# Two-piece expert passes regrouped by array width, down weights moved from a copy to a DMA, scatters and last sums rearranged

## The reference

```python
logits = h @ gate_w.T
scores = softmax(logits); topk_w, topk_idx = top_k(scores, 6)
for e in range(16):
    g = h @ w_gate[e].T          # 256 -> 176
    u = h @ w_up[e].T
    out = silu(g) * u @ w_down[e].T   # 176 -> 256
    y = y + cw[:, e:e + 1] * out
```

## Time and profile before

| | us |
|---|---|
| median of 3 runs (lowest to highest) | 876.45 (874.01 to 876.85) |
| the profiled execution, whole | 867.91 |
| its span (first to last instruction) | 866.1 |
| first pass of the last stage begins (T of pass 2) | 638.70 |
| last `pair_y` ends | 846.46 |

### The profile page before, as it was taken

How to read it: one execution, slowest core, us unless ns; L and a number is a source line. 1 busy time by engine, 2 the same in 40 slices (tenths; PEclk the granted TensorE clock), 3 DMA queues, 4 the chain that set the end, 5 groups by cost and what they waited for, 6 DMA issues and landing times.

```text
span 866.1 us, 15945 instructions
## 1 busy us (share of the span) xinstructions
PE 789.5 (91%) x5107; PEld 521.6 (60%) x5107; DVE 507.1 (59%) x1270; ACT 400.1 (46%) x856; POOL 278.8 (32%) x374
## 2 busy tenths in 40 slices
PE   5988799889979998999999999899899999999990
PEld 3566566676557785777777767667654444444440
DVE  5999876666512236756556655777534763443564
ACT  3987777555123333443233342232527454555540
POOL 3643744113500033111111111137602265554430
PEclk9998999999989999999999999999979999999995
DMA  4002770181253221044453533113232243537316
GB/s 140 2 1 37 244 257 2 35 238 51 80 165 109 86 67 56 19 142 134 134 159 122 171 92 78 53 50 101 90 68 68 62 126 116 135 117 245 101 46 212
DMA packets 103590, 91.22 MB, mean 105 GB/s; under 512 B 38104, under 2 KB 95448, under 8 KB 103512
## 3 DMA queue, kind: packets, MB, share of 16 engines
q1 hardware_dynamic: 93288, 67.92, 27.2%
q0 software_dynamic: 6912, 19.28, 6.4%
q10 hardware_dynamic: 3312, 3.02, 1.0%
HBM read 50.47 MB, written 38.67 MB: 103 GB/s over the span
## 4 chain that ended last, share of the span: by engine, by line
PE 62%; DVE 12%; issue 6%; POOL 5%; DMA 4%; ACT 3%; DVEq 0%; ACTq 0%; SPq 0%; POOLq 0%
PE bank L1383 8%; PE bank L1346 7%; PE bank L673 7%; PE bank L1240 6%; PE bank L1226 5%; PE bank L699 5%; PE bank L896 3%; PE bank L2166 3%; POOL rows L771 3%; PE bank L918 2%; PE bank L657 2%; PE bank L2123 2%; PE bank L2150 2%; DMA rows<-arena,sidx 2%; PE bank L685 2%
## 5 line engine op out<-in xcount | busy, mean ns | idle before, releaser
L1487 ACT ACTIVATE arena<-bank 128x512 f32<-128x512 f32 (+1 forms) x96 | 46.9, 525 | 147.5 <-PE bank L1346 147.4
L1138 POOL TENSOR_TENSOR arena<-arena,causal_t 128x256 f32<-128x256 f32 x64 | 45.1, 726 | 214.0 <-ACT arena L1492 214.0
L781 POOL DMA_INDIRECT ret<-arena,ridx x64 | 66.1, 1033 | 103.9 <-ACT arena L747 49.9
L673 PE MATMUL bank<-arena 128*64 (+1 forms) x512 | 91.0, 477 | 1.0 <-DVE arena L733 1.0
L1383 PEld LDWEIGHTS bank<-arena 128*128 128x128 f32 x640 | 76.6, 192 | 5.2 <-POOL arena L1138 2.7
L1383 PE MATMUL bank<-arena 128*128 128x129 f32 x640 | 77.5, 276 | 1.7 <-POOL arena L1138 1.7
L1346 PE MATMUL bank<-arena 128*128 128x512 f32 (+3 forms) x256 | 75.7, 440 | 1.4 <-DVE arena L1546 1.4
L699 PE MATMUL bank<-arena 88*64 (+1 forms) x512 | 69.8, 393 | 3.2 <-DVE arena L725 1.7
L754 DVE TENSOR_TENSOR arena<-arena,bank 128x176 f32<-128x176 f32 x64 | 21.6, 337 | 86.2 <-ACT arena L741 86.0
L1240 PE MATMUL bank<-arena 128*128 128x256 f32 x256 | 62.6, 389 | 1.5 <-DVE arena L1553 1.5
L1240 PEld LDWEIGHTS bank<-arena 128*128 128x128 f32 x256 | 49.4, 194 | 22.6 <-issue 12.1
(11 more groups left out here) (288 smaller groups left out, 1527.0 us busy)
## 6 DMA issues: line engine op xcount, KB each, us to landing
rows<-arena SPq DMA_DIRECT2D x16, 544.0 KB, 4.6
rows_in<-place SPq DMA_DIRECT2D x5, 1664.0 KB, 14.4
arena<-rows SPq DMA_DIRECT2D x64, 128.0 KB, 2.1
arena<-in_w_gu SPq DMA_DIRECT2D x24, 256.0 KB, 3.5
arena<-ret SPq DMA_DIRECT2D x12, 512.0 KB, 6.7
arena<-in_w_dn SPq DMA_DIRECT2D x24, 176.0 KB
arena<-in_wq SPq DMA_DIRECT2D x32, 128.0 KB, 3.9
arena<-in_wo SPq DMA_DIRECT2D x32, 128.0 KB, 2.0
```

Of the source, the lines that this page charges most:

```text
L673: mm = nc.tensor.matmul(p_gu[J % 2][u * HR:(u + 1) * HR, 0:2 * FE].rearrange("p (y n) -> p y n", y=2), pxT[:, J % 2, k, u * HR:(u + 1) * H ...
L781: nc.gpsimd.indirect_dma_start(ret[h], bass.IndirectOffsetOnAxis(ap=ridx[:, h, j:j + 1], axis=0), py[J % NY], None).then_inc(s_ret, 16)
L1138: nc.gpsimd.tensor_tensor(blocks, blocks, causal_t[:].unsqueeze(1).to_broadcast([P, 2, P]), ALU.mult).then_inc(s_p, 1)
L1487: nc.scalar.activation(th[:, sbank * 512:sbank * 512 + w], b_s[sbank][:, 0:w], ACT.Tanh, scale=SCALE / SOFTCAP).then_inc(s_th, 1)
```

## The change

Six edits belong to it:

1. The PE order of pass J becomes `T(J+2), H(J-1), G(J+1), D(J-1)`: the two transposing groups stand together and the two 64-wide groups stand together. DVE's order becomes `pair_h(J-1), pair_mul(J+1), pair_y(J-1)`, then the routing part.
2. `pair_copy_dn` is gone. `load_dn_pair` on SP loads the second piece's down weights from HBM (176 KB), with the row number read from the table, four steps behind `load_rows`.
3. `pair_y` moves from ACT to DVE. Most routing parts of half 1 are called one pass earlier.
4. `send_rows` takes ranges: half 0 sends five scatters in each of heads 25 to 28 and four in head 29 (was four in each of heads 25 to 30). Half 1 sends groups of six (was four).
5. `rows1_back(0)` moves from pass 1 into head 31, ahead of `pair_x(0)`.
6. Of the last sums, tiles 0 and 1 stay as `add_back` on DVE. For tiles 2 and 3 DVE builds 12 diagonal matrices (`spread_weights`, passes 40 to 45), and PE sums with them in PSUM (`sum_back`); DVE then adds that to x.

```diff
         def rows1_table(self, dve, h):
...
-            for y, w in enumerate((GU1, 2 * DIM)):
-                nc.vector.tensor_scalar(tab1[:, h, y, :], c.ej, float(E1 - 1), float(w), ALU.min, ALU.mult).then_inc(s_tab, 1)
+            nc.vector.tensor_scalar(tab1[:, h, 0, :], c.ej, float(E1 - 1), float(GU1), ALU.min, ALU.mult).then_inc(s_tab, 1)
+            for u, w in enumerate((2 * DIM, FE)):
+                nc.vector.tensor_scalar(tab1[:, h, 1, :].rearrange("p (j u) -> p u j", u=2)[:, u, :],
+                                        c.ej.rearrange("p (j u) -> p u j", u=2)[:, u, :], float(E1 - 1), float(w),
+                                        ALU.min, ALU.mult).then_inc(s_tab, 1)
...
-            pe.wait_ge(s_wbd, J + 1)
+            pe.wait_ge(s_wbd[J % 2], wbd_0[J % 2] + 16 * (J // 2 + 1))
...
-        def pair_y(self, act, J):
+        def pair_y(self, dve, J):
...
-            nc.scalar.copy(py[J % NY], p_y).then_inc(s_pye, 1)
+            nc.vector.tensor_copy(py[J % NY], p_y).then_inc(s_pye, 1)
...
+        def spread_weights(self, dve, k):
+            if k == 0:
+                dve.wait_ge(s_rows, SC + 2 * SC1)
+            for t in (2, 3):
+                ins = nc.vector.scalar_tensor_tensor(out=dg[:, 2 * k + t - 2, :], in0=ident[:], scalar=wk1[:, 1, k, t:t + 1],
+                                                     in1=ident[:], op0=ALU.mult, op1=ALU.mult)
+        def sum_back(self, pe):
+            pe.wait_ge(s_rx1, 3)
+            for k in range(K1):
+                pe.wait_ge(s_ys[k], ys_0[k] + 32)
+                for t in (2, 3):
+                    mm = nc.tensor.matmul(b_y[0][:, (t - 2) * DIM:(t - 1) * DIM], dg[:, 2 * k + t - 2, :], ys[k][:, t, :],
+                                          start=(k == 0 and t == 2), stop=(k == K1 - 1), skip_group_check=True)
+        def load_dn_pair(self, sp, J):
+            off = self.owner(sp, J, 1, 1)
+            if J >= 2:
+                sp.wait_ge(s_pyd, NB + J - 1)
+            back = io["w_dn1"].rearrange("i p d -> (i p) d")
+            sp.dma_start(wbd[0:HB, J % 2, :].rearrange("p (q d) -> p q d", q=2),
+                         back[bass.ds(off, FE), :].rearrange("(q p) d -> p q d", p=HB)).then_inc(s_wbd[J % 2], 16)
...
-            for J in range(2 * NP1):
-                self.load_rows(sp, J)
-                if J % NP1 == 1:
+            for J in range(2 * NP1 + 4):
+                if J < 2 * NP1:
+                    self.load_rows(sp, J)
+                if J >= 4:
+                    self.load_dn_pair(sp, J - 4)
+                if J in (1, NP1 + 1):
...
-                sp.wait_ge(s_xres.sem, 18 + 2 * q)
+                sp.wait_ge(s_xres.sem, 18 + q)
...
-                if 25 <= n < 31:
-                    self.send_rows(pool, 0, (n - 25,))
+                if 25 <= n < 30:
+                    self.send_rows(pool, 0, 5 * (n - 25), min(5 * (n - 24), 4 * K1))
...
-                    self.send_rows(pool, 1, range(K1))
+                    for t in range(4):
+                        self.send_rows(pool, 1, t * K1, (t + 1) * K1)
...
                 if J + 2 < 2 * NP1:
                     self.pair_turn(pe, J + 2)
+                if J:
+                    self.pair_hidden(pe, J - 1)
+                if J == 4:
+                    pe.wait_ge(s_xres.sem, 12)
+                    self.ln_turn(pe, 10)
+                    self.ln_turn(pe, 11)
+                if J == 1:
+                    self.turn(pe, NH - 1)
+                if J == 5:
+                    self.logits(pe, 3)
+                if J == 11:
+                    self.places1(pe, 1)
+                if J == 2:
+                    self.project(pe, NH - 1)
                 if J + 1 < 2 * NP1:
                     self.pair_gate_up(pe, J + 1, offs[J + 1])
                 if J + 3 < 2 * NP1:
                     offs.append(owners(J + 3))
-                self.pair_hidden(pe, J)
                 if J:
                     self.pair_down(pe, J - 1, offs[J - 1])
...
+            self.pair_hidden(pe, 2 * NP1 - 1)
             self.pair_down(pe, 2 * NP1 - 1, offs[2 * NP1 - 1])
+            self.sum_back(pe)
...
                 if n == NH - 1:
+                    self.rows1_back(dve, 0)
                     self.pair_x(dve, 0)
...
             for J in range(2 * NP1):
+                if J:
+                    self.pair_h(dve, J - 1)
+                if J == 1:
+                    self.turned(dve, NH - 1)
                 if J + 1 < 2 * NP1:
                     self.pair_mul(dve, J + 1)
-                self.pair_h(dve, J)
-                self.pair_copy_dn(dve, J)
...
                 if J == 2:
                     dve.wait_ge(s_y, NH)
                     self.residual(dve, 4, b_y[0])
                     self.residual(dve, 6, b_y[1])
+                if J:
+                    self.pair_y(dve, J - 1)
...
-            for i in range(4 * K1):
-                self.add_back(dve, 1, i)
+            self.pair_h(dve, 2 * NP1 - 1)
+            self.pair_y(dve, 2 * NP1 - 1)
+            for i in range(4 * K1):
+                if i % 4 < 2:
+                    self.add_back(dve, 1, i)
+            dve.wait_ge(s_y, NH + 1)
+            self.residual(dve, 6, b_y[0])
```

More of the change, by code:

```diff
@@ L705, in owner @@
             if q == u:
-                eng.wait_ge(s_tab, 3 + 2 * (h + 1))
-            return eng.value_load(tab1[0:1, h, y, q:q + 1], min_val=0, max_val=(E1 - 1) * (GU1, 2 * DIM)[y])
+                eng.wait_ge(s_tab, 3 + 3 * (h + 1))
+            step = (GU1, (2 * DIM, FE)[u])[y]
+            return eng.value_load(tab1[0:1, h, y, q:q + 1], min_val=0, max_val=(E1 - 1) * step)
         def pair_copy_gu(self, act, J):
@@ L760, in pair_h, with send_rows @@
             nc.vector.tensor_copy(phT[0:HB, J % 2, :, :], p_h[0:HB, :].rearrange("p (q n) -> p q n", q=2)).then_inc(s_pte, 1)
-        def send_rows(self, pool, h, groups):
-            for g in groups:
-                if g == 0:
-                    pool.wait_ge(s_pl, DI1[h])
-                    pool.wait_ge(ln_xn, NT + 20 + 4 * h)
-                    pool.wait_ge(s_zf, ZF1)
-                else:
-                    pool.wait_ge(s_rows, SC + SC1 * h + 64 * g)
-                for i in range(4 * g, 4 * g + 4):
-                    nc.gpsimd.indirect_dma_start(rows1[h], bass.IndirectOffsetOnAxis(ap=sidx1[:, h, i % K1, i // K1:i // K1 + 1], axis=0),
-                                                 xa[h][:, i // K1, :], None).then_inc(s_rows, 16)
+        def send_rows(self, pool, h, lo, hi):
+            if lo == 0:
+                pool.wait_ge(s_pl, DI1[h])
+                pool.wait_ge(ln_xn, NT + 20 + 4 * h)
+                pool.wait_ge(s_zf, ZF1)
+            else:
+                pool.wait_ge(s_rows, SC + SC1 * h + 16 * lo)
+            for i in range(lo, hi):
+                nc.gpsimd.indirect_dma_start(rows1[h], bass.IndirectOffsetOnAxis(ap=sidx1[:, h, i % K1, i // K1:i // K1 + 1], axis=0),
+                                             xa[h][:, i // K1, :], None).then_inc(s_rows, 16)
         def send_back(self, pool, J):
@@ L1512, in act @@
                     self.pair_silu(act, J + 1)
-                if J:
-                    self.pair_y(act, J - 1)
-                if J == 3:
+                if J == 2:
                     self.ln_std(act, 10)
                     self.ln_std(act, 11)
-                if J == 5:
+                if J == 4:
                     self.ln_evac(act, 10)
                     self.ln_evac(act, 11)
-                if J == 6:
+                if J == 5:
                     self.exps(act, 3)
-            self.pair_y(act, 2 * NP1 - 1)
         def mul(self, dve, M):
@@ L1691, in dve @@
                     self.residual(dve, 6, b_y[1])
+                if J:
+                    self.pair_y(dve, J - 1)
+                if J == 2:
                     self.ln_stats(dve, 10)
+                    self.ln_stats(dve, 11)
                 if J == 3:
-                    self.ln_stats(dve, 11)
-                if J == 4:
                     self.ln_norm(dve, 10)
                     self.ln_norm(dve, 11)
+                if J == 5:
+                    self.route_a(dve, 3)
                 if J == 6:
-                    self.route_a(dve, 3)
-                if J == 7:
                     self.route_b1(dve, 3)
-                if J == 9:
+                if J == 8:
                     self.route_b2(dve, 3)
+                if J == 10:
+                    self.route_b3(dve, 3)
                 if J == 11:
-                    self.route_b3(dve, 3)
-                if J == 12:
                     self.rows1_read(dve, 1)
@@ L1710, in dve @@
                     self.rows1_weights(dve, 1)
-                if J == 14:
+                if J == 15:
                     self.rows1_edges(dve, 1)
-                if J == 15:
+                if J == 16:
                     self.rows1_table(dve, 1)
-                if J == 16:
+                if J == 17:
                     self.rows1_owner(dve, 1)
```

(2 more changed lines are left out.)

35 lines of the change are left out of this document (8 added, 27 removed).

## The result

| | before | changed |
|---|---|---|
| median us (runs, lowest to highest) | 875.23 (4, 873.9 to 876.85) | 905.78 (4, 901.88 to 907.12) |
| ratio, 95% interval | | 1.0341 (1.03 to 1.0382) |
| span of the profiled execution, us | 866.1 | 905.0 |
| T(2) starts | 638.70 | 639.46 |
| last `pair_y` ends | 846.46 | 886.65 |

A forecast was written before the change was run, and what follows sets the result against it. TensorE was taken to bound the kernel, at 3.07 us per steady pass. Terms -17.7 + 19.6 - 5.4 + 7.5 + 2.7 - 0.8 = +5.9 on the median 876.45 gave 882.3 us, range 871 to 888.

The forecast's parts named there:

- clock term: Behind the wait at pass 47: PE's clock falls afterwards, costing +2.7 us, ends 0 and +3.5.
- Stalls 27.1: Passes 2 to the last: PE waits for DVE's parts, 27.1 us in place of 7.5, so +19.6.
- edit 1, pass length: Steady PE pass: two width changes instead of four give 2.77 us for 3.07, -17.7 over 61 passes.
- wait at pass 47: Down-weight load for pass 47 queues behind the DMAs of `load_back(0)` and stalls D: +7.5 us, ends +5 and +8.5.
- T(2), edit 5: Start of the passes: T of pass 2 at 633.3 in place of 638.70, -5.4 us, ends -6 and -3.
- room of 0.70 us: Steady pass, new order: a DVE part of e us stalls PE by e - 0.70, where before it had over 3 us.
- 2.4 us of pass 2: Pass 2: residuals ahead of `pair_y` and both `ln_stats` behind it stall PE by 2.4 us.
- rival by which DVE's parts stay hidden: Routing passes: room over 3 us as before, stalls 7.5 us, 2 given back to the scatter chain: 864.7 us, chance 12%.
- The 2 us wait of before is within the 7.5: Scatter stage near pass 28: the old 2 us wait for a result buffer already counts in the 7.5 us of waits.
- the one that had the load not held up: Pass 47: small loads pass the 3 MB, so +7.5 and +2.7 go: 872.1 us, chance 12%.
- the one that had the stall short: Pass 47: a stall of 3 us and 1.3 for the clock: 876.4 us, no change, chance 12%.
- regrouping brings nothing: Steady PE passes: the new order of groups saves no time: 900 us, chance 3%.

The follow-up runs named there:

- e18: Changed kernel with each of the 24 scatters of half 1 waiting until the one before has landed, on the chip of e17: 919.58 us.
- e17: Changed kernel unaltered, run once more for a profile on the chip of e18: 903.15 us, ratio 1.0311.
- e4: Kernel before the change, unaltered, run for a second profile: 878.77 us.
- e3: Changed kernel with `pair_h` on ACT instead of DVE and two PSUM banks for D's result from pass 8 on: 895.1 us, ratio 1.0193.
- e5: e2 with D one pass later and two PSUM banks for D's result from pass 8 on: 885.09 us, ratio 1.0105.
- e10: e5 with a second bank for H's result, the head edits, and the first routing parts in their old passes: 871.39 us, ratio 0.9949.
- e12: Kernel before with `rows1_back(0)` moved into head 31, half 0's scatters by fives and the head edits: 869.36 us, ratio 0.9925.
- e6: Changed kernel with PE reading the first passes' registers in the heads and `pair_x(0)` ahead of `rows1_back(0)`: 898.33 us, ratio 1.0274.
- e2: Changed kernel with the six DMAs of `load_back(0)` issued one at a time, two passes apart: 895.13 us, ratio 1.0204.
- e14: e10 with two PSUM banks for T's result from pass 16 on: 852.65 us, ratio 0.9846.
- head edits: Registers of the first passes read in the heads, `pair_x(0)` ahead of `rows1_back(0)`; alone on the changed kernel (e6) 898.33 us.
- e13_fill: Changed kernel with idle PE products ahead of D in seven passes, sized to stay under its waits: 888.87 us, ratio 1.0246.
- e11: Changed kernel with half 1's 24 scatters cut to rows of 64 bytes, written to a scratch: 904.67 us, ratio 1.0321.

## Why the prediction was wrong

The step that failed is the price of a wait. The forecast gave one wait a clock term (+2.7 behind pass 47) and gave none to the waits for DVE's parts. "Stalls 27.1" was a sum of bare idle times. Measured, half clock took 18.9 us between T(2) and T(63): 3.3 behind pass 47, 8.9 in the routing stretches and 6.7 in those of the scatters. That a wait brings it down was in the rows: 0.52 behind 5.85 us in the earlier trace rows, which the forecast used once, and it says itself that the clock fell behind the 3.26 of the earlier trace rows. That waits of 1.6 to 2.6 us do it too was in no row of before. This step is half of the miss; results that come late, which no row of before showed, and the head start are most of the rest.

| term | forecast | measured in the profiled execution |
|---|---|---|
| edit 1, pass length | -17.7 | -17.1 (61 x 0.28) |
| PE's waits for DVE's parts | 27.1 | 20.4: 14.5 up to index, 2.9 for the later parts (e18, and 0.8 for `rows1_back`), 2.7 in the last two passes, 0.3 for `add_back` |
| wait at pass 47 | +7.5 | +8.65 |
| half clock | +2.7 | +18.9 |
| late results, beyond DVE's parts | not considered | 10.9 (the waits of the stretches 16 to 39, 14.84, less 2.90 and 1.08 for a load) |
| T(2), edit 5 | -5.4 | +0.8 (-0.8 in e17 against e4) |
| last sums, edit 6 | -0.8 | -1.3 (18.35 behind the last `pair_y` for 19.64) |

Between the two profiles it closes so: 0.8 for T(2), -17.1 for edit 1, 54.0 for the losses (64.5 less 10.5), 2.5 from T(63) to the last `pair_y` and -1.3 for the last sums are 38.9. That is 33 us over the forecast. Half clock is 16.2 of them, late results 10.9, T(2) 6.2; DVE's parts were forecast 6.7 too high, and the rest are smaller terms.

- **Edit 1 and DVE's room** were right as mechanisms. The room of 0.70 us gave 3.93 for 4.1 (`route_b1`), 1.55 for 1.8 (`route_b2`), 2.72 for 3.4 (index), and 0.76 for 1.0 (weights, in e18, where no late result covers it). The 2.4 us of pass 2 didn't come: there PE has `project(31)` to do. The 16 passes from 2 to 17 took 80.8 us for some 70 forecast. The rival by which DVE's parts stay hidden is ruled out by the waits for L757. e3, e5 and e10 show the order as the cause, though none gets back to the 8.2 us that the routing stretches lost before (19.2, 23.9 and 14.2).
- **The scatter stage.** "The 2 us wait of before is within the 7.5" was read off an execution without late results. With late results the old order itself loses 13 us there (e4 and e12, on two chips). The change loses 23; that a late H or D now has G's 1.24 us of cover instead of a pass is the likely reason, argued from the order and not tested by itself. The first scatter came at 703.5 and not near 690.
- **The head start** missed by 4 to 6 us. I took 1.7 us for register reads; six in a row ahead of G took 3.83, and `rows1_back(0)` ahead of `pair_x(0)` 0.89. e6 shows both. "T(1) 627.7" was also 1.8 us early in this execution because the last head began later.
- **Edit 2** came out as forecast: hidden in steady passes, and stuck behind `load_back(0)` (e2). Of the rivals, the one that had the load not held up and the one that had the stall short are wrong. No run shows the stall of 3 us that the latter takes: the bare wait at pass 47 took 8.65 us, and 8.4 to 9.3 in the other runs that have it.
- **The rival "regrouping brings nothing", 900**, came nearest in time by luck and is wrong in mechanism: the pass did get shorter (2.79 for 3.07), and where no result came late e14 kept 9.75 us of it.

Between the medians the change costs 30.5 us, between the two profiles 38.9: the first profile of before had no late results, which is worth some 11 us (13.3 less 2.3).

## What to carry to other kernels

Price a wait of PE as idle time plus what PE does at half clock behind it: here 38 us of waits brought 19 more (15 behind 39.5 in e17). Filling one wait with idle products took its part away, but the clock then fell behind other waits, so a single filled wait need not pay. A regrouping that puts producer and consumer into one pass buys width changes with slack; give each intermediate result a second bank and a pass of distance first, and then regroup (with the head edits 0.995 where results come late, 0.985 where they don't, instead of 1.034). Hold that against the cheap part alone: the head edits in the old order gave 0.9925. Take a second profile before trusting a stage in which transfers and scatters are dense: one execution without late results made the old order look 11 us better covered than it is.

## What the runs showed of the hardware

- The clock falls behind waits of 1.6 to 4 us too, not only behind one of 5.9: after a wait of 1.59 us at 692.34 the stretch lost 3.0 us to half clock (0.52 from 692.34 to 698.64), while the same wait in e17_after lost none (1.00 from 690.78 to 694.20). After the 2.55 us at 657.24 it was 0.57 up to 662.65. Which of such waits drops it varied from run to run. At two waits e13_fill shows that PE's idle time is the cause: filled, they left the clock at 1.00 (673.96 to 676.74 and 819.62 to 823.42), while bare, in the changed kernel, it was 0.54 behind `route_b1` (677.81 to 682.75) and 0.50 behind pass 47 (836.23 to 841.00).
- PE's results reached DVE, ACT and SP up to 5 us late (5.1 in e10_spaced) while POOL issued indirect DMAs every 1.27 us, on four of five chips, and with rows of 64 bytes the time stayed (e11); with pauses between the scatters (one every 2.7 us and more) none was late (e18). The mechanism stays open.
- Six DMAs of 512 KB in a row made SP's own issues long: 5.18 us for the six, then 1.82 for one of 128 KB. Issued one at a time (e2) one of 512 KB takes SP 0.38.
